# The places of some raw tiles' splits and loads in the first, sixth, seventh and ninth period, and the seventh rotation of down weights one period up, in a fused conditioning, attention and FFN kernel

## The chip, the cores and the metric

One core of one Trainium2 chip. The metric is the device time of one execution in microseconds (us). The kernel before took 1590.42 us, the median of three executions (1587.31, 1590.42 and 1590.79).

## The reference

Four sequences of 512 tokens with 512 channels go through two blocks. `_bi_wkv` is a recurrence over the tokens in both directions, `_L0_attn_ref` an attention by segments with a memory of 128 x 128 per head, `_L0_ffn_ref` a gated FFN whose hidden vector is rotated by a Hadamard transform.

```python
x = x + attn(bi_wkv(x, fside, fside, w, u, cond), Wq, Wk, Wv, Wo, betas)
x = x + ffn(bi_wkv(x, fside, fside, w2, u2, cond), W1, W2, W3)
# bi_wkv: two scans a = a*decay + exp(k)*v and b = b*decay + exp(k) forward, two backward,
#         out = sigmoid(r) * num / den * gain
# attn, per head (16, of 128) and segment (128 tokens):
scores = where(causal_mask, q @ k.T / scale, -inf)
att_dot = softmax(scores) @ v
att_mem = sigma_q @ mem / (sigma_q @ z)
delta = v - sigma_k @ mem / (sigma_k @ z)
mem, z = mem + sigma_k.T @ delta, z + sum(sigma_k)
out = (beta * att_mem + (1 - beta) * att_dot) @ Wo
# ffn: hidden = fwht(silu(x @ W1.T) * (x @ W3.T)); out = hidden @ W2.T
```

## The kernel before

Every engine has its own program, written out by hand; semaphores tie them together. The order inside an engine's program is fixed, so an instruction that waits holds all behind it on that engine.

**Periods.** The attention is a loop over n = 0 to 31 (sequence n // 8, pair of heads n % 8). One turn n is the period n + 1 of this text: n = 0 is the first period, n = 5 the sixth, n = 29 the 30th. In a period TensorE (PE) turns keys and makes scores (`turn_k`, `scores`), turns the attention of the period before (`turn_att`), updates and reads the memory (`update`, `recall`), multiplies probabilities by values (`pv`), and in between multiplies out values (`v_block`, rows `psG<-parts,yh`) and the keys and queries of the next period (`kq_part`, rows `psG<-yh,parts`). Every fourth period (n = 4, 8, ...) is a burst, in which the projection by Wo is made too (`wo`, rows with `ah`).

**Raw tiles.** fp32 products are made in three passes of a high and a low part. The weights come as a stream `STREAM` of tiles of 128 x 1024. The first time that a tile is needed it is loaded raw, in two halves of 256 KB, into `stage` (four buffers, so two tiles; SP, `load_half`), the high part is made by ACT (`split_hi`, L1702; for some tiles by POOL, L2211), the low part by POOL (`split_w`, L2213), and SP saves both (`keep`, `high_k<-parts` and the like). Later uses load the saved parts (`load_w`, `parts<-high_v` and the like, 512 KB each). Tiles lie in a ring of seven places; a load or a split waits (`wait_used`) until PE has used the tile before in its place and its save has landed. `split_hi(upto)`, `split_w(upto)`, `load_w(upto)` and `keep(upto)` go on in the stream up to tile `upto`; `ENDS[n]` is the end of period n's part of it. Tile 4 is the key weight for n = 2 (called k2 here), tile 30 a value weight for n = 8 and 9 (v9), tile 32 a key weight (k8), tiles 40 to 43 are Wo tiles (o12 to o15), tiles 46 and 47 are the value weights that the tenth period uses first (w10, w11), tile 48 a key weight (k10, the keys of n = 10, made in the tenth period).

**Work behind.** Each period has eight slots (`behind(n, k)`). A table `STEPS`, cut by `shared_out` with costs and rooms, says which steps of the recurrence (scans on VectorE, DVE; `yh`: high part of its output by ACT, low part `yl` by POOL) and which of the eight rotations of the down weights fall into which slot. A rotation i loads HA (`load`), adds and subtracts on DVE (`lv0` to `lv3`), makes high and low part HH (ACT, L1776) and HL (DVE, L1238) in `hi` and `lo`, multiplies by a Hadamard matrix on PE (`mult`, function `hadamard`, four matmuls, L872 and L873), copies the result to HO and stores it (ACT, `out_w2`). HH, HL and HO have one buffer each. `hadamard(i)` waits for HH and HL of i, and for the copies of i - 1.

**Waits that the prediction speaks of.** `v_block(0, half, 0)` writes PSUM bank G[half] and waits until ACT has read the queries of n = 1 out of it: `w.wait_ge(a_qm, 2 + half + 1)`, which `relu_kq(1, "q", half, ...)` (L1880) counts up. The value blocks of the seventh period (n = 6, called SWAPPED) are the first for the second sequence and wait for all its `yh` and `yl`.

Of the kernel before, what the change touches and what calls it, by code (L numbers as in the profile page):

```python
# [65 lines left out]
STEPS = [(name, t, cost) for t in range(4, NA) for name, cost in SCAN]  # L66
STEPS += [("hstart", 0, 3000)]
for _i in range(8):
    for name, cost in HADAMARD:
        if name != "mult":  # L70
            STEPS.append((name, _i, cost))
        elif _i > 0:
            if _i == 2:
                STEPS += [(z, 0, c) for z, c in MODULATE[1:]]
            STEPS.append((name, _i - 1, cost))
            if _i == 1:
                STEPS.append(MODULATE[0][:1] + (0, 0))
# [75 lines left out]
SWAPPED = 6  # L153
# [157 lines left out]
def adaln_attn_ffn(nc, xT_d, fT_d, wu_d, wq_d, wk_d, wv_d, wo_d, betas_d,  # L311
# [9 lines left out]
    with ExitStack() as ctx:  # L321
# [1363 lines left out]
        def scalar(e):  # L1685
# [103 lines left out]
            def out_w2(i):  # L1789
                for j in range(2):  # L1790
                    cut = slice(512 * j, 512 * j + 512)
                    w.wait_ge(pe_h, 2 * i + j + 1)
                    w.wait_ge(d_ho, 16 * i)
                    e.activation(HO[:, cut], X[j][:, :], ACT.Copy, scale=RSQ).then_inc(a_ho, 1)
                w.wait_ge(a_ho, 2 * i + 2)
                e.dma_start(w2_s[i].rearrange("p a d -> p (a d)"), HO[:, :]).then_inc(d_ho, 16)
# [10 lines left out]
            def behind(n, k):  # L1807
                for name, i, _ in STEPS[at[0]:UPTO[n, k]]:
                    if name == "nf":
                        load_k(i + 2 if i + 2 < NA else NT)  # L1810
                    elif name == "er":
                        exp_r(i)
                    elif name == "ek":
                        exp_k(after(i))
                    elif name == "eu":
                        exp_u(after(i))
                    elif name == "rc1":
                        load_r(i)
                    elif name == "yh":
                        high_y(i)  # L1820
                        keep_ratio(i)
                    elif name == "hi":
                        high_w2(i)
                        if i == 7:
                            out_w2(6)
                    elif name == "load":
                        load_w2(i)
                    elif name == "mult" and i != 6:
                        out_w2(i)
                    elif name == "zsig":  # L1830
                        z_sigmoid(i)
                    elif name in ("z0", "z1", "z2", "z3"):
                        z_high(i, int(name[1]))
                at[0] = UPTO[n, k]
# [22 lines left out]
            def copy_kq(n, kind, j, bank):  # L1857
                w.wait_ge(pe_k if kind == "k" else pe_q, 2 * n + j + 1)
                w.wait_ge(pe_s, 2 * (n - 1) + j + 1)
                if n == 0:  # L1860
                    w.wait_ge(v_oy, 4)
                e.activation((kT if kind == "k" else qT)[:, j, :], bank[:, :], ACT.Copy).then_inc(  # L1862
                    a_kc if kind == "k" else a_qc, 1)
# [135 lines left out]
            for n in range(NN):  # L1999
                nx, burst = n + 1, is_burst(n)  # L2000
                more = nx < NN
                end, o = ENDS[n], ENDS[n] - 10
# [19 lines left out]
                exp_s(n, 1)  # L2022
                behind(n, 1)
                if n in (SWAPPED, NN - 2):
                    copy_kq(nx, "k", 0, G[0])
                    exp_kq(nx, "k", 0, G[0])
                elif more and not bare:
                    copy_v(n, 0)
                elif not more:
                    sigmoid(0, 0, G[0])  # L2030
# [3 lines left out]
                    exp_u(4)  # L2034
                if burst:
                    copy_v(n, 1)
                if n == SWAPPED:
                    behind(n, 3)
                split_hi(o + 3 if burst else 3 if n == 0 else end if more else end + 1)
                behind(n, 3)  # L2040
                if n == SWAPPED:
# [34 lines left out]
                        copy_kq(nx, "k", j, G[j])  # L2076
                        exp_kq(nx, "k", j, G[j])
                if more:
                    split_hi(5 if n == 0 else end + (3 if n == 3 else 1 if burst else 2))
                    copy_kq(nx, "q", 0, G[0])  # L2080
                    exp_kq(nx, "q", 0, G[0])
                    if n not in (0, 4):
                        split_hi(end + (4 if n == 3 else 3 if burst else 2))
                    copy_kq(nx, "q", 1, G[1])
                    if n == 0:
                        exp_kq(nx, "q", 1, G[1])
                    if n == 4:
                        split_hi(end + 3)
                else:
                    high_h(0, 0)  # L2090
                    high_h(0, 1)
# [100 lines left out]
        def gpsimd(e):  # L2192
# [133 lines left out]
            for n in range(NN):  # L2326
                nx, burst = n + 1, is_burst(n)
                more = nx < NN
                end, o = ENDS[n], ENDS[n] - 10
                if n >= LATE_V:  # L2330
                    scale_v(n)
                behind(n, 0)
                if n > 0:
                    split_w(o + 2 if burst else end + 1 if n == 3 else end - 1 if more else end)
                behind(n, 1)
                behind(n, 2)
                if n == 0:
                    ekv(4)
                    euv(4)
                if n == SWAPPED:  # L2340
                    behind(n, 3)
                split_w(o + 3 if burst else 3 if n == 0 else end if more else end + 1)
                behind(n, 3)
                if burst:
                    split_w(o + 5)
                behind(n, 4)
                split_w(o + 8 if burst else 4 if n == 0 else end + 2 if n == 3 else end + 1 if more else end + 2)
                behind(n, 5)
                if more and n != 4 and nx < LATE_V:
                    scale_v(nx)  # L2350
                if burst:
                    split_w(end)
                if n == 4:
                    scale_v(nx)
                behind(n, 6)
                if burst:
                    split_w(end + 2)
                if more:
                    split_w(5 if n == 0 else end + (4 if n == 3 else 3 if burst else 2))
                else:  # L2360
                    low_h(0, 0)
                    low_h(0, 1)
                behind(n, 7)
# [49 lines left out]
        def sync(e):  # L2413
# [110 lines left out]
            for n in range(NN):  # L2524
# [27 lines left out]
                keep(o + 5 if burst else end + 2 if n == 3 else end)  # L2552
                load_w(o + 9 if burst else 6 if n == 0 else end + (5 if n == 3 else 3))
                behind(n, 5)
                if burst:
                    keep(o + 8)
                    load_w(o + 11)
# [5 lines left out]
                    load_w(o + 13)  # L2563
                if more:
                    keep(5 if n == 0 else end + (4 if n == 3 else 2 if burst else 1))
                    load_w(end + (6 if n == 3 else 4))
                behind(n, 7)
            def load_x(b):
                w.wait_ge(d_x1[b], 16)
# [107 lines left out]
```

## Time and profile before

| | |
|---|---|
| median of three executions | 1590.42 us |
| the profiled execution | 1587.02 us |
| its span | 1585.2 us |
| PE busy | 1542.9 us (97%), 8854 matmuls |
| DVE, ACT, POOL busy | 1214.6 (77%), 781.1 (49%), 615.5 us (39%) |
| prologue, 0 to 60.38 us | PE busy 33.10 us |
| 32 periods, 60.38 to 1068 us | PE busy 997.15 of 1007.62 us |
| FFN, 1068 to 1585.2 us | PE busy 512.67 of 517.20 us |

The span is from the first to the last instruction; 1.8 us of the profiled time lie around it. A period lasts 26 to 29 us, a burst some 49. Matmuls overlap, so PE's busy time is that of the union; a matmul of 512 columns starts 0.23 us after the one before it at full clock. Where PE is idle the timeline says how long before an instruction, and which event came last.

### The profile page before, as it was taken

To read this page: it belongs to the slowest core of one execution; us is meant where nothing else is said; L and a number is where in the kernel's file an instruction comes from. 1 tells how busy PE (TensorE), PEld (TensorE's weight loads), DVE (VectorE), ACT (ScalarE), POOL (GpSimd) and SP (SyncE) were. 2 spreads that over 40 slices of the span, in tenths; PEclk is the share of its full clock that TensorE was granted. 3 is DMA by queue.
4 is the path that set the end of the run, shared out by engine and by line. 5 is a ranking of instruction groups with operands and counts; after the bars stand their busy time and mean duration, and the time that the engine had idled before them with its cause. 6 is when DMAs were issued, how large, how long until landed. Compare 5 with 4: busy or idle time off the path is not lost.

```text
span 1585.2 us, 25420 instructions
## 1 busy us (share of the span) xinstructions
PE 1542.9 (97%) x8854; PEld 1342.2 (85%) x8854; DVE 1214.6 (77%) x2718; ACT 781.1 (49%) x1687; POOL 615.5 (39%) x433
## 2 busy tenths in 40 slices
PE   4899999999999999999999999999999999999999
PEld 2678998898898898898889889889888888888887
DVE  8869968888878778888765764665897888687785
ACT  3556655645526535644645562662554443344442
POOL 3647646262211113222101010143664465666662
PEclk9999999999999999999999999999999999999999
DMA  5357677577485386386278658347211122311111
GB/s 176 123 194 249 236 280 250 195 288 297 176 294 181 134 300 226 113 304 226 97 268 332 209 196 325 103 168 254 90 59 53 58 90 73 107 43 64 54 41 54
DMA packets 113407, 276.62 MB, mean 175 GB/s; under 512 B 11648, under 2 KB 36608, under 8 KB 111872
## 3 DMA queue, kind: packets, MB, share of 16 engines
q1 hardware_dynamic: 94416, 241.96, 42.3%
q10 hardware_dynamic: 18864, 33.04, 6.7%
q8 instruction: 71, 1.16, 0.3%
q14 instruction: 56, 0.46, 0.1%
HBM read 226.71 MB, written 48.25 MB: 173 GB/s over the span
## 4 chain that ended last, share of the span: by engine, by line
PE 88%; DVE 6%; issue 2%; DMA 2%; ACT 1%; POOL 1%; SPq 0%; ACTq 0%; POOLq 0%; DVEq 0%
PE psG L664 16%; PE psG L666 16%; PE psG L665 16%; PE psX L664 4%; PE psX L852 3%; PE psX L665 3%; PE psX L666 3%; PE psX L807 3%; PE psZ L833 3%; PE psZ L824 2%; PE psZ L832 2%; PE psZ L665 2%; PE psY L665 2%; PE psZ L666 2%; PE psZ L664 2%
## 5 line engine op out<-in xcount | busy, mean ns | idle before, releaser
L2213 POOL TENSOR_TENSOR parts<-stage,parts 128x512 fp32r<-128x512 f32 x160 | 235.2, 1492 | 143.0 <-ACT parts L1702 140.6
L664 PE MATMUL psG<-yh,parts 128*128 128x512 f32 x646 | 263.0, 407 | 0.0
L666 PE MATMUL psG<-yh,parts 128*128 128x512 f32 x646 | 253.0, 392 | 0.0
L665 PE MATMUL psG<-yl,parts 128*128 128x512 f32 x646 | 251.8, 390 | 0.0
L2281 POOL TENSOR_TENSOR vs<-v,omb 128x512 f32<-128x512 f32 x64 | 92.9, 1474 | 386.2 <-PE psX L807 210.4
L666 PEld LDWEIGHTS psG<-yh,parts 128*128 128x128 f32 x646 | 121.2, 188 | 26.7
L664 PEld LDWEIGHTS psG<-yh,parts 128*128 128x128 f32 x646 | 121.7, 188 | 21.8 <-issue 0.4
L665 PEld LDWEIGHTS psG<-yl,parts 128*128 128x128 f32 x646 | 121.8, 189 | 21.4
L664 PE MATMUL psG<-ah,parts 128*128 128x256 f32 x448 | 127.1, 284 | 0.2 <-POOL parts L2213 0.2
L665 PE MATMUL psG<-al,parts 128*128 128x256 f32 x448 | 125.2, 280 | 0.0
L666 PE MATMUL psG<-ah,parts 128*128 128x256 f32 x448 | 124.8, 279 | 0.0
L1702 ACT ACTIVATE parts<-stage 128x512 fp32r<-128x512 f32 x152 | 88.0, 623 | 55.1 <-DMA stage<-in_w 15.8
L1862 ACT ACTIVATE kT<-psG 128x512 f32<-128x512 f32 x62 | 37.0, 596 | 152.2 <-PE psG L666 150.8
L1212 DVE RECIPROCAL DBK<-DF 128x128 f32<-128x128 f32 x120 | 107.3, 926 | 0.6
L664 PE MATMUL psG<-parts,yh 128*128 128x512 f32 x240 | 101.1, 421 | 6.5 <-ACT etmp L1880 3.7
L1910 ACT ACTIVATE S<-S,st 128x128 f32<-128x128 f32 x256 | 99.0, 391 | 8.1 <-issue 5.5
L1295 DVE CUSTOM_DVE_ANT_0 S<-psX,mask 128x128 f32<-128x128 f32 x256 | 57.8, 286 | 55.9 <-PE psX L807 55.9
L1307 DVE TENSOR_TENSOR mem<-psZ,mem 128x129 f32<-128x129 f32 x192 | 47.8, 287 | 64.1 <-PE psZ L824 64.1
L666 PE MATMUL psG<-parts,yl 128*128 128x512 f32 x240 | 95.1, 396 | 0.0
L665 PE MATMUL psG<-parts,yh 128*128 128x512 f32 x240 | 94.1, 392 | 0.0
L2289 POOL TENSOR_TENSOR hl<-sg,hh 128x512 fp32r<-128x512 f32 x36 | 51.0, 1416 | 91.8 <-ACT hh L1960 91.8
L664 PEld LDWEIGHTS psG<-ah,parts 128*128 128x128 f32 x448 | 84.2, 188 | 0.4 <-issue 0.3
(279 smaller groups left out, 4241.3 us busy)
## 6 DMA issues: line engine op xcount, KB each, us to landing
parts<-high_o SPq DMA_DIRECT2D x52, 512.0 KB, 6.1
parts<-low_o SPq DMA_DIRECT2D x52, 512.0 KB, 7.6
parts<-high_v SPq DMA_DIRECT2D x36, 512.0 KB, 4.8
parts<-low_v SPq DMA_DIRECT2D x36, 512.0 KB, 6.4
stage<-in_w SPq DMA_DIRECT2D x64, 256.0 KB, 3.0
parts<-high_k SPq DMA_DIRECT2D x23, 512.0 KB, 5.5
parts<-low_k SPq DMA_DIRECT2D x23, 512.0 KB, 6.3
parts<-high_q SPq DMA_DIRECT2D x23, 512.0 KB, 4.5
```

Of the source, the lines that this page charges most:

```text
L664: e.matmul(out, lh, rh, start=first, stop=False, skip_group_check=check)
L665: e.matmul(out, lh, rl, start=False, stop=False, skip_group_check=check)
L666: return e.matmul(out, ll, rh, start=False, stop=last, skip_group_check=check)
L807: m = e.matmul(X[j][:, seg(s)], qT[:, j, seg(s)], kT[:, j, seg(s)], start=True, stop=True)
L1212: e.reciprocal(dbk[:, 128 * j:128 * j + 128], df[:, 128 * j:128 * j + 128]).then_inc(v_rc, 1)
L1295: m = e.tensor_tensor_reduce(S[:, j, seg(s)], X[j][:, seg(s)], mask[:, :], -SCALE, -NEG, ALU.add, ALU.min, st[:, 1, j, s:s + 1])
L1307: e.tensor_tensor(mem[:, j, 0:P + 1], Z[j][:, 258:387], mem0[:, 0:P + 1] if s == 0 else mem[:, j, 0:P + 1], ALU.add).then_inc(v_mem, 1)
L1702: e.activation(hi, raw, ACT.Copy).then_inc(a_wh, 1)
L1910: m = e.activation(S[:, j, seg(s)], S[:, j, seg(s)], ACT.Exp, bias=st[:, 1, j, s:s + 1], scale=-1.0, accum_out=st[:, 2, j, s:s + 1])
L2213: e.tensor_tensor(lo, raw, hi, ALU.subtract).then_inc(p_wl, 1)
L2281: e.tensor_tensor(vs[:, :, j, :].rearrange("p (a b) d -> p a b d", a=2), pick(v[:, :, :, j, 0:P], *HALVES[n]), omb[:, 128 * j:128 * j + 12 ...
L2289: e.tensor_tensor(hl[u % 2][:, j, :], hid(k)[:, :], hh[u % 2][:, j, :], ALU.subtract).then_inc(p_hl, 1)
```

## The change

Four places. (1) First period: ACT splits tile 4 (k2) after the queries of n = 1 are copied out of PSUM, where it did it before them. (2) Sixth and seventh period: ACT and POOL split tile 30 (v9) at the end of the sixth instead of amid the seventh, SP loads tile 32 one place earlier, POOL's `EUV` comes after that split, and in the seventh (and the 31st) ACT does slot 2's work (there `yh` and the last HH) before it copies keys out of PSUM. (3) Ninth period: SP issues the loads of w10 and w11 between saves of the Wo tiles instead of after all four. (4) `mult` of rotation 6 moves from slot 1 of the 31st period to slot 3 of the 30th, with `out_w2(6)`; the steps of rotation 7 that followed (`load`, `lv0` to `lv2`) move one slot back, `lv3` stays.

```diff
@@ -66,10 +66,12 @@
 STEPS = [(name, t, cost) for t in range(4, NA) for name, cost in SCAN]
 STEPS += [("hstart", 0, 3000)]
 for _i in range(8):
+    if _i == 7:
+        STEPS.append(("mult", 6, 300))
     for name, cost in HADAMARD:
         if name != "mult":
             STEPS.append((name, _i, cost))
-        elif _i > 0:
+        elif 0 < _i < 7:
             if _i == 2:
                 STEPS += [(z, 0, c) for z, c in MODULATE[1:]]
             STEPS.append((name, _i - 1, cost))
@@ -1821,11 +1823,9 @@
                         keep_ratio(i)
                     elif name == "hi":
                         high_w2(i)
-                        if i == 7:
-                            out_w2(6)
                     elif name == "load":
                         load_w2(i)
-                    elif name == "mult" and i != 6:
+                    elif name == "mult":
                         out_w2(i)
                     elif name == "zsig":
                         z_sigmoid(i)
@@ -2022,6 +2022,7 @@
                 exp_s(n, 1)
                 behind(n, 1)
                 if n in (SWAPPED, NN - 2):
+                    behind(n, 2)
                     copy_kq(nx, "k", 0, G[0])
                     exp_kq(nx, "k", 0, G[0])
                 elif more and not bare:
@@ -2034,8 +2035,6 @@
                     exp_u(4)
                 if burst:
                     copy_v(n, 1)
-                if n == SWAPPED:
-                    behind(n, 3)
                 split_hi(o + 3 if burst else 3 if n == 0 else end if more else end + 1)
                 behind(n, 3)
                 if n == SWAPPED:
@@ -2076,16 +2075,17 @@
                         copy_kq(nx, "k", j, G[j])
                         exp_kq(nx, "k", j, G[j])
                 if more:
-                    split_hi(5 if n == 0 else end + (3 if n == 3 else 1 if burst else 2))
+                    if n > 0:
+                        split_hi(end + (3 if n == 3 else 1 if burst else 2))
                     copy_kq(nx, "q", 0, G[0])
                     exp_kq(nx, "q", 0, G[0])
                     if n not in (0, 4):
-                        split_hi(end + (4 if n == 3 else 3 if burst else 2))
+                        split_hi(end + (4 if n == 3 else 3 if burst or n == 5 else 2))
                     copy_kq(nx, "q", 1, G[1])
                     if n == 0:
                         exp_kq(nx, "q", 1, G[1])
-                    if n == 4:
-                        split_hi(end + 3)
+                    if n in (0, 4):
+                        split_hi(5 if n == 0 else end + 3)
                 else:
                     high_h(0, 0)
                     high_h(0, 1)
@@ -2337,8 +2337,6 @@
                 if n == 0:
                     ekv(4)
                     euv(4)
-                if n == SWAPPED:
-                    behind(n, 3)
                 split_w(o + 3 if burst else 3 if n == 0 else end if more else end + 1)
                 behind(n, 3)
                 if burst:
@@ -2356,7 +2354,7 @@
                 if burst:
                     split_w(end + 2)
                 if more:
-                    split_w(5 if n == 0 else end + (4 if n == 3 else 3 if burst else 2))
+                    split_w(5 if n == 0 else end + (4 if n == 3 else 3 if burst or n == 5 else 2))
                 else:
                     low_h(0, 0)
                     low_h(0, 1)
@@ -2552,6 +2550,10 @@
                 keep(o + 5 if burst else end + 2 if n == 3 else end)
                 load_w(o + 9 if burst else 6 if n == 0 else end + (5 if n == 3 else 3))
                 behind(n, 5)
+                if n == 8:
+                    load_w(o + 11)
+                    keep(o + 6)
+                    load_w(o + 12)
                 if burst:
                     keep(o + 8)
                     load_w(o + 11)
@@ -2563,7 +2565,7 @@
                     load_w(o + 13)
                 if more:
                     keep(5 if n == 0 else end + (4 if n == 3 else 2 if burst else 1))
-                    load_w(end + (6 if n == 3 else 4))
+                    load_w(end + (6 if n == 3 else 5 if n == 5 else 4))
                 behind(n, 7)
             def load_x(b):
                 w.wait_ge(d_x1[b], 16)
```

On ACT, at the end of the first period, before (stage0 and stage1 hold k2; qT, etmp0 and etmp1 belong to the queries of n = 1):

```order
L1702 ACTIVATE parts<-stage0 128x512
L1702 ACTIVATE parts<-stage1 128x512
L1862 ACTIVATE qT<-psG0 128x512
L1880 ACTIVATE etmp0<-psG0 128x512
L1871 ACTIVATE etmp0<-etmp0 128x512
L1862 ACTIVATE qT<-psG1 128x512
L1880 ACTIVATE etmp1<-psG1 128x512
L1871 ACTIVATE etmp1<-etmp1 128x512
L1720 ACTIVATE ER<-ER 128x512
```

and in the change:

```order
L1862 ACTIVATE qT<-psG0 128x512
L1880 ACTIVATE etmp0<-psG0 128x512
L1871 ACTIVATE etmp0<-etmp0 128x512
L1862 ACTIVATE qT<-psG1 128x512
L1880 ACTIVATE etmp1<-psG1 128x512
L1871 ACTIVATE etmp1<-etmp1 128x512
L1704 ACTIVATE parts<-stage0 128x512
L1704 ACTIVATE parts<-stage1 128x512
L1722 ACTIVATE ER<-ER 128x512
```

Two splits moved from ahead of six instructions to behind them; ER is still last.

On ACT, across the border of the sixth and the seventh period, before (stage0 and stage1 hold v9; `ah`, `bet`, `omb` and S belong to the seventh):

```order
L1910 ACTIVATE S,st<-S,st 128x128 x4
L1702 ACTIVATE parts<-stage0 128x512
L1702 ACTIVATE parts<-stage1 128x512
L1910 ACTIVATE S,st<-S,st 128x128 x4
L1862 ACTIVATE kT<-psG0 128x512
L1880 ACTIVATE etmp0<-psG0 128x512
L1871 ACTIVATE etmp0<-etmp0 128x512
L1768 ACTIVATE yh1<-OY 128x512
L1745 DMA kx0<-in_fT 128x512
L1862 ACTIVATE kT<-psG1 128x512
```

and in the change:

```order
L1910 ACTIVATE S,st<-S,st 128x128 x8
L1770 ACTIVATE yh1<-OY 128x512
L1862 ACTIVATE kT<-psG0 128x512
L1880 ACTIVATE etmp0<-psG0 128x512
L1871 ACTIVATE etmp0<-etmp0 128x512
L1747 DMA kx0<-in_fT 128x512
L1862 ACTIVATE kT<-psG1 128x512
```

The two splits are gone from here (they stand ahead of `qT<-psG1`, ten instructions earlier), and yh stands ahead of the three instructions on psG0.

On PE in the 31st period, before, the four matmuls of rotation 6 with one row on either side (`psZ1<-v,kn` ends `update`, psG1 is the second half of the next keys):

```order
L824 MATMUL psZ1<-v,kn 128x129
L872 MATMUL psX0<-HH,had 128x512
L873 MATMUL psX0<-HL,had 128x512
L872 MATMUL psX1<-HH,had 128x512
L873 MATMUL psX1<-HL,had 128x512
L664 MATMUL psG1<-yh1,parts 128x512
```

On PE in the 30th period, between `recall` of the second segment and the second half of a value block, in the change:

```order
L834 MATMUL psZ1<-mem,sk 128x129
L835 MATMUL psZ1<-mem,sq 128x129
L874 MATMUL psX0<-HH,had 128x512
L875 MATMUL psX0<-HL,had 128x512
L874 MATMUL psX1<-HH,had 128x512
L875 MATMUL psX1<-HL,had 128x512
L666 MATMUL psG1<-parts,yh1 128x512
L667 MATMUL psG1<-parts,yh1 128x512
L668 MATMUL psG1<-parts,yl1 128x512
```

The four matmuls of rotation 6 have left the 31st period, where `psG1<-yh1,parts` now follows `psZ1<-v,kn` at once, and stand behind `recall` and ahead of the value block.

## Rows read from the trace of the kernel before

**Rows 1.** waits of PE, whole span: us in total, times, longest
```profile
PE psG L664 <- ACT etmp L1880: 3.7, 1, 3.7
...
PE psG L664 <- POOL yl L2238: 2.5, 1, 2.5
PE psX L872 <- DVE HL L1238: 1.3, 1, 1.3
```

**Rows 2.** timeline of PE, first period: start, us, what [idle before]
```profile
81.59 0.39 PE L666 MATMUL psG<-yh,parts 128*128 128x512 f32 x1
85.71 0.58 PE L664 MATMUL psG<-parts,yh 128*128 128x512 f32 x1 [3.73 <-ACT etmp L1880]
...
89.43 0.39 PE L664 MATMUL psG<-parts,yh 128*128 128x512 f32 x1
```

**Rows 3.** windows: us; PE, PEld, DVE, ACT, POOL busy; PEclk; DMA; GB/s
```profile
85.70:89.50 3.80, 3.79 (x10) 2.98 (x11) 0.00 (x0) 2.65 (x5) 1.42 (x3) 0.55 0.96 357
```

**Rows 4.** timeline of ACT, end of the first period
```profile
82.69 0.63 ACT L1702 ACTIVATE parts<-stage 128x512 fp32r<-128x512 f32 x1 [4.98 <-DMA stage<-in_wk]
```

**Rows 5.** timeline of DVE, first and second period
```profile
80.65 1.70 DVE L1365 SCALAR_TENSOR_TENSOR sk<-kT,etmp 128x512 f32<-128x512 f32 x1
...
96.33 0.69 DVE L1365 SCALAR_TENSOR_TENSOR sq<-qT,etmp 128x512 f32<-128x512 f32 x1
...
100.27 0.46 DVE L1307 TENSOR_TENSOR mem<-psZ,mem 128x129 f32<-128x129 f32 x2
```

**Rows 6.** timeline of POOL, end of the first period
```profile
91.71 1.29 POOL L2213 TENSOR_TENSOR parts<-stage,parts 128x512 fp32r<-128x512 f32 x1
```

**Rows 7.** timeline of PE, second and seventh period
```profile
100.74 0.38 PE L832 MATMUL psZ<-mem,sk 128*128 128x129 f32 x2
...
260.96 0.47 PE L664 MATMUL psG<-parts,yh 128*128 128x512 f32 x1 [2.50 <-POOL yl L2238]
```

**Rows 8.** timeline of ACT, seventh period
```profile
248.31 0.60 ACT L1862 ACTIVATE qT<-psG 128x512 f32<-128x512 f32 x1 [0.99 <-PE psG L666]
...
256.71 0.57 ACT L1862 ACTIVATE kT<-psG 128x512 f32<-128x512 f32 x1
...
258.33 0.61 ACT L1768 ACTIVATE yh<-OY 128x512 fp32r<-128x512 f32 x1
```

**Rows 9.** timeline of POOL, seventh period
```profile
254.91 3.47 POOL L2213 TENSOR_TENSOR parts<-stage,parts 128x512 fp32r<-128x512 f32 x2 [5.33 <-ACT parts L1702]
259.02 1.68 POOL L2238 TENSOR_TENSOR yl<-OY,yh 128x512 fp32r<-128x512 f32 x1 [0.63 <-ACT yh L1768]
```

**Rows 10.** timeline of PE, 30th and 31st period
```profile
1001.18 0.47 PE L664 MATMUL psG<-parts,yh 128*128 128x512 f32 x1
...
1026.01 0.39 PE L664 MATMUL psG<-yh,parts 128*128 128x512 f32 x1
...
1029.73 0.47 PE L872 MATMUL psX<-HH,had 128*128 128x512 f32 x1 [1.28 <-DVE HL L1238]
```

**Rows 11.** timeline of DVE, 30th and 31st period
```profile
1001.78 1.23 DVE L1238 TENSOR_TENSOR HL<-HA,HH 128x1024 fp32r<-128x1024 f32 x1 [3.05 <-ACT HH L1776]
...
1028.41 1.23 DVE L1238 TENSOR_TENSOR HL<-HA,HH 128x1024 fp32r<-128x1024 f32 x1 [2.64 <-ACT HH L1776]
```

**Rows 12.** timeline of ACT, 31st period
```profile
1025.70 0.58 ACT L1862 ACTIVATE kT<-psG 128x512 f32<-128x512 f32 x1
...
1027.33 1.04 ACT L1776 ACTIVATE HH<-HA 128x1024 fp32r<-128x1024 f32 x1
```

**Rows 13.** timelines of PE, tenth period, and of SP, ninth period
```profile
355.28 0.47 PE L664 MATMUL psG<-parts,yh 128*128 128x512 f32 x1 [0.22 <-issue]
...
362.24 0.40 PE L664 MATMUL psG<-yh,parts 128*128 128x512 f32 x1
...
344.15 1.00 SPq L2455 DMA_DIRECT2D parts<-low_k  x1
```

**Rows 14.** DMA issues, 343.7 to 346 us: count, KB, us to landing
```profile
parts<-low_k SPq DMA_DIRECT2D x1, 512.0 KB, 15.1
```

## Prediction

> **What bounds the kernel now.** I read the page first: PE is busy for 1542.9 of 1585.2 us, so only what PE waits for can be won. Next the waits of PE over the whole span: behind the prologue there are three above 1 us, one each, of 3.7, 2.5 and 1.3 us [rows 1]. Then the timelines of PE around these three, to see where they lie, and of ACT, POOL and DVE at the same times, to see what each engine did instead. The first lies at the end of the first period [rows 2], the second in the seventh [rows 7], the third in the 31st [rows 10]. The change touches just these places, and the ninth period, where the next one has a wait of 0.22 us [rows 13]. All else that follows is tied to PE's progress, so I let later work move along with PE.
>
> **A, first period.** PE's last matmul on the queries of n = 1 starts at 81.59 and the value block behind it at 85.71, released by etmp [rows 2]. That is ACT's relu of these queries, and ACT stood before it at the first raw half of k2: 4.98 us idle until its DMA landed, and 82.69 when it began [rows 4]. With the splits behind the queries' six instructions, ACT takes half 0 as soon as PE has made it. The second half of the queries is 12 matmuls of 0.23 us, so half 0 is ready near 79.1; a copy and a relu of 0.6 us each make it free at 80.3, before PE gets there at 81.82. For half 1 ACT can copy at 82.0; its relu also waits for sk, DVE's op of 1.70 us from 80.65, done at 82.35 [rows 5]; it ends near 83.2, and PE comes to half 1 at 81.82 + 12 x 0.23 = 84.6. So the wait goes whole: 85.71 - 81.82 = 3.9 us. Behind the wait the granted clock was 0.55 of full on the mean of 85.7 to 89.5, that is mostly its lower level of 1.2 GHz [rows 3]: nine starts took 89.43 - 85.71 = 3.72 us [rows 2], where nine at 0.23 and a first one 0.1 longer take 2.17. Without 3.73 us of idleness before it I expect no fall of the clock: another 1.55 us. A is worth -5.4 us.
>
> What pays for it: k2 is split about 1 us later (behind ACT's exp of half 1, near 83.7, not at 82.69), and PE begins the second period 5.4 us earlier. k2 and q2 are used only in the middle and at the end of the second period. But POOL's last low part of q2, at 91.71 to 93.0 [rows 6], ended before DVE's sq at 96.33 (0.69 us). Now it runs at about 90.2 to 91.5 (POOL no longer waits for ER there), and sq comes at 96.33 - 5.4 = 90.9. The like op at 80.65 took 1.70 us, with POOL busy beside it [rows 5]. So sq and all behind it on DVE are late by between 0 and 1.0 us; I take the overlap, 0.5. DVE's mem begins at 100.27 and takes 0.46 for two halves, the first done near 100.5, and PE reads it at 100.74 [rows 5, 7]: 0.2 us of slack, so PE waits 0.3 us, between 0 and 0.8. Estimate +0.3. The Trainium skill, SBUF — State Buffer, section "SBUF: two separate sides", says that DVE and GpSimd share a port pair as an exclusive lock, whichever starts first holding it for its whole instruction. By that rule sq waits out POOL's op and runs 0.5 us late, and by the nearest row 1.0 us; the wait of PE would be 0.3 or 0.8.
>
> **B, seventh period.** The value block begins at 260.96 behind 2.50 us of idleness, released by yl [rows 7]. POOL made yl from 259.02, when yh had come, and yh stood at 258.33 behind ACT's three instructions on the keys, which began at 256.71 [rows 8, 9]. POOL itself was at v9 until 254.91 + 3.47 = 258.38. Now both are out of the way: v9's two splits on ACT leave (1.04 us earlier), and yh goes first, at 256.71 - 1.04 = 255.7. It is done at 256.3, yl at 256.3 + 1.3 to 1.7 = 257.6 to 258.0, and PE wants it at 260.96 - 2.50 - 0.16 (matmuls overlap) = 258.3. The keys' relu, which the block waits for too, ends near 257.5. So the wait goes whole, -2.6 us, between -2.2 and -2.66.
>
> The split that moved costs ACT 1.04 us ahead of q1's copy at 248.31, before which ACT was idle for 0.99 [rows 8]: 0.05 us, for which scores of half 1 would wait, hidden by those of half 0 (0.9 us). POOL's v9 now ends near 251; then EUV, needed in slot 7 only. No cost. If v9's raw halves landed later than 247.2, ACT and with it q1, scores and all of the seventh period would wait for them one for one.
>
> **C, rotation 6.** In the 30th period PE would now do the four matmuls at the place of the row at 1001.18. They wait for HL of 6, which DVE makes from 1001.78 to 1003.01, being itself released by HH on ACT [rows 10, 11]. Nothing in the change makes this earlier: HH stands behind the copies of rotation 5 and a value copy. PE's idleness there is new: 1003.1 - 1001.3 = 1.8 us (the like place in the 31st began 0.09 after HL ended). In the 31st period the four matmuls (1.0 us) are gone, so PE reaches rotation 7 at 1028.3 - 1.0 = 1027.3 in the old time. HH of 7 now goes ahead of the keys' copies, at 1025.70 and not 1027.33 [rows 12], so HL is ready at 1029.64 - 1.63 = 1028.0, and PE waits 0.7 us where it waited 1.3. Sum: 1.8 + 0.7 - 1.3 = +1.2 us. Bounds: 0 if HL of 6 were early enough, 2.0 if the order on ACT brings nothing. Behind the waiting matmuls in the 30th stand the value block and turn_p; ACT and DVE wait for these but have slack of 0.8 us and more, so nothing is added. A clock fall is not counted: the wait of 2.50 us had none behind it (0.47 us for its first matmul, as ever) [rows 7].
>
> **D, ninth period.** The block at 355.28 waits 0.22 us for w10 and w11 [rows 13]. w11 now has two saves of 1 MB less ahead of it, so it comes earlier and the 0.22 goes: -0.3 us with the overlap. The Trainium skill, DMA: Bandwidth & Descriptors, section "Queues, rings and completion order", says that descriptors are consumed in ring order; that is why issuing earlier helps, and the sum would be the same without it.
>
> **Sum:** -5.4 + 0.3 - 2.6 + 1.2 - 0.3 = -6.8 us. Against the profiled execution, 1587.0, that is 1580.2 (span 1578.4). The median shown is 3.4 us higher, 1590.4, and gives 1583.6; two of four executions lie at 1587 and two at 1590.6. I put 1583.0.
>
> **Rivals.** (1) As summed, -5 to -8.8: 0.63. (2) Part of A and B is given back: the clock falls all the same, or POOL, DVE or transfers in the second to fifth period don't follow PE by 5.4 us. For it speaks that DVE is full there and its op grew from 0.69 to 1.70 us beside POOL [rows 5]; against it, that PE hardly waits there now. Worth 1.6 (clock) + 2 = 3.6: -3.2 us, 0.2; a quarter of it within 0.2%. (3) The change doesn't do what it says: v_block waits for something else at 82 us, as the split v3 whose low part is POOL's. Then A is nearly 0: -1.5 us, 0.08, and no change to be measured. (4) The other side: in the ninth period the loads between the saves hold up SP. w11 waits for the save of o12, and saves of o14 and o15 and the load of k10 stand behind it. k10's low part was issued at 344.15 and took 15.1 us [rows 13, 14], landing at 359.3; PE uses it at 362.24 [rows 13], 2.9 us of slack. Each us beyond costs one; it takes 6.8 + 3.2 + 2.9 = 13 us of delay before the kernel is slower by 0.2%. The bytes ahead of k10 are the same, so I expect none; 0.05, at +4 us. (5) C costs nothing and all else holds: -8.0, 0.04.
>
> **Numbers.** 0.2% (3.2 us) is about what a measurement of this kernel can tell from no change. Faster by more: 0.63 + 0.15 + 0.04 = 0.82; within: 0.05 + 0.08 = 0.13; slower: 0.05. The range goes from the profiled time less 8.4 (1578.6) to the median less 2.8 (1587.6); what lies outside is (3), (4) and the tails.
>
> **What would show it.** PE's wait for etmp gone and PEclk 1.00 from 80 to 90 us; no wait for yl near 250; a new wait for HL of 1.8 us near 994 and one of 0.7 near 1021; none for `issue` near 347; mem L1309 as releaser in the second period with 0.3 us. Wrong would be: k2 landing so late that POOL runs into DVE's chain for more than 1 us, or a wait for transfers in the tenth period.

## The result, and the profile after

The changed kernel takes 1579.93 us (median of 5 runs, 1579.76 to 1580.68). The kernel before, in the same comparison, takes 1590.42 us (5 runs, 1587.31 to 1590.79). The ratio is 0.994, with a 95% interval of 0.9926 to 0.9955: faster by 0.6%, an effect under 2% but clear of 1. The time forecast was 1583.0 us, with a range of 1578.6 to 1587.6; the time lies inside, 3.1 us below the forecast. The profiled execution took 1580.52 us with a span of 1578.7 us, where the sum of the prediction had 1580.2 and 1578.4.

A period is counted here from the first matmul of one period's first block to that of the next, so that the lengths and the prologue add up, but for the last stretch, to the span. From the two timelines of PE:

| stretch | before, us | after, us | change | foretold |
|---|---|---|---|---|
| prologue | 60.38 | 60.01 | -0.37 | nothing |
| 1st period | 32.46 | 26.89 | -5.57 | -5.4 |
| 2nd | 26.08 | 26.61 | +0.53 | +0.3 |
| 7th | 28.84 | 26.10 | -2.74 | -2.6 |
| 10th | 26.58 | 26.09 | -0.49 | -0.3 |
| 15th | 26.38 | 27.21 | +0.83 | nothing |
| 30th and 31st | 27.02 + 24.00 | 29.83 + 22.37 | +1.18 | +1.2 |
| span | 1585.2 | 1578.7 | -6.5 | -6.8 |

The waits of PE in the kernel after, over the whole span (us in total, times, longest); these answer to [rows 1]:

```profile
PE psX L874 <- issue: 2.3, 2, 1.7
PE psZ L834 <- DVE mem L1309: 1.9, 5, 0.8
```

The waits of 3.7 us for etmp and 2.5 us for yl are gone. In their place stand two at the Hadamard matmuls (line 874, that was 872) and a longer list for mem. The timeline of PE after shows them one by one (start, duration, and in brackets the idle time before):

```profile
95.22 0.49 PE L834 MATMUL psZ<-mem,sk 128*128 128x129 f32 x2 [0.27 <-DVE mem L1309]
...
505.37 0.49 PE L834 MATMUL psZ<-mem,sk 128*128 128x129 f32 x2 [0.85 <-DVE mem L1309]
...
995.37 0.47 PE L874 MATMUL psX<-HH,had 128*128 128x512 f32 x1 [1.68 <-issue]
...
1023.19 0.47 PE L874 MATMUL psX<-HH,had 128*128 128x512 f32 x1 [0.59 <-issue]
```

The window of 80 to 90 us after (us; PE, PEld, DVE, ACT, POOL busy; PEclk; DMA share; GB/s) is full, at full clock, where the kernel before had 0.55 behind its wait [rows 3]:

```profile
80.00:90.00 10.00, 10.00 (x61) 8.74 (x60) 4.79 (x19) 5.79 (x13) 7.21 (x9) 1.00 0.86 311
```

ACT at the end of the first period after, against [rows 4]: the queries' copy and relu stand at once behind PE, and the splits of k2 come last.

```profile
78.92 0.60 ACT L1862 ACTIVATE qT<-psG 128x512 f32<-128x512 f32 x1 [1.42 <-PE psG L668]
79.41 0.59 ACT L1880 ACTIVATE etmp<-psG 128x512 f32<-128x512 f32 x1
...
82.15 0.59 ACT L1880 ACTIVATE etmp<-psG 128x512 f32<-128x512 f32 x1
...
83.32 1.14 ACT L1704 ACTIVATE parts<-stage 128x512 fp32r<-128x512 f32 x2
```

POOL and DVE in the second period after, against [rows 5, 6]: sq starts 0.58 us after POOL's low part of q2 and takes 1.26 us, not 0.69. mem is late by as much as its slack doesn't cover, and PE waits 0.27 us.

```profile
89.81 1.30 POOL L2213 TENSOR_TENSOR parts<-stage,parts 128x512 fp32r<-128x512 f32 x1
```

```profile
90.39 1.26 DVE L1367 SCALAR_TENSOR_TENSOR sq<-qT,etmp 128x512 f32<-128x512 f32 x1
...
94.91 0.46 DVE L1309 TENSOR_TENSOR mem<-psZ,mem 128x129 f32<-128x129 f32 x2
```

In the seventh period after, yh and yl are early enough (against [rows 8, 9], which had them at 258.33 and 259.02 in a period that began 5.4 us later in the span):

```profile
250.33 0.61 ACT L1770 ACTIVATE yh<-OY 128x512 fp32r<-128x512 f32 x1
```

```profile
251.02 1.29 POOL L2238 TENSOR_TENSOR yl<-OY,yh 128x512 fp32r<-128x512 f32 x1 [4.35 <-ACT yh L1770]
```

In the 30th and 31st period after, each Hadamard matmul starts 0.1 us behind the end of HL, though the view names only "issue" as its releaser; the timeline of DVE (against [rows 11]) says what was really late:

```profile
994.04 1.22 DVE L1240 TENSOR_TENSOR HL<-HA,HH 128x1024 fp32r<-128x1024 f32 x1 [3.05 <-ACT HH L1778]
...
1021.86 1.23 DVE L1240 TENSOR_TENSOR HL<-HA,HH 128x1024 fp32r<-128x1024 f32 x1 [1.03 <-ACT HH L1778]
```

On SP in the ninth period after, w11's load is issued at 334.35, ahead of two saves, and k10's low part at 339.65 (against [rows 13]); no wait follows in the tenth:

```profile
334.35 0.32 SPq L2452 DMA_DIRECT2D parts<-high_v  x1
...
339.65 0.68 SPq L2453 DMA_DIRECT2D parts<-low_k  x1
```

### The profile page after: what moved, and what is told of

Its sections match the earlier page's. It is cut to its first block, busy times and chain, and to the rows that moved or that the text cites. A ratio compares the mean times of both kernels' runs of the same rounds, so it can differ in the third digit from the quotient of the medians.

```text
span 1578.7 us, 25420 instructions
## 1 busy us (share of the span) xinstructions
PE 1542.7 (98%) x8854; PEld 1341.6 (85%) x8854; DVE 1217.6 (77%) x2718; ACT 781.4 (49%) x1687; POOL 614.3 (39%) x433
## 4 chain that ended last, share of the span: by engine, by line
PE 89%; DVE 6%; issue 2%; ACT 1%; DMA 1%; POOL 0%; ACTq 0%; SPq 0%; DVEq 0%; POOLq 0%
PE psG L666 16%; PE psG L668 16%; PE psG L667 16%; PE psX L854 4%; PE psX L666 4%; PE psX L668 3%; PE psX L667 3%; PE psX L809 3%; PE psZ L835 3%; PE psZ L826 3%; PE psZ L834 2%; PE psY L667 2%; PE psZ L667 2%; PE psZ L668 2%; PE psZ L666 2%
```

## The experiments

Two questions stood after this. One is whether the four parts have the prices of the table. The other is why the medians differ by 10.5 us where the two profiled executions differ by 6.5. Experiments 1 to 4 put one part each into the kernel before. Their times are compared with 30 executions of it (median 1588.42 us, 1585.42 to 1591.06).

**1. Part A alone.** The splits of k2 behind the queries on ACT:

```diff
-                    split_hi(5 if n == 0 else end + (3 if n == 3 else 1 if burst else 2))
+                    if n > 0:
+                        split_hi(end + (3 if n == 3 else 1 if burst else 2))
...
-                    if n == 4:
-                        split_hi(end + 3)
+                    if n in (0, 4):
+                        split_hi(5 if n == 0 else end + 3)
```

> Of the change, the part in the first period alone (k2 split behind the queries). Own theory: the wait for etmp and the low clock behind it go, a wait of 0.3 us for mem comes in the second period; span 1585.2 - 5.6 + 0.4 = 1580.0 us, ratio 0.9965 or lower. Rival, that part of the gain is given back in the second to fifth period: span 1582 or more. Second question: the median of the kernel before (1590.4) lies 3.4 us above its profiled execution, while the changed kernel's executions lie within 0.9 us; if the spread comes from the wait in the first period, it is gone here (executions within 1 us, median near 1582).

Measured: 1583.74 us (6 runs, 1582.56 to 1585.3), ratio 0.9972 (0.9961 to 0.9983). First period 26.90 us, second 26.60: as expected. But the span was 1581.5, only 3.7 below that of before, since its seventh period took 30.38 us and not 28.84, with the same wait for yl before it. The timeline of PE of this kernel:

```profile
255.97 0.76 PE L664 MATMUL psG<-parts,yh 128*128 128x512 f32 x1 [2.49 <-POOL yl L2239]
```

The wait is that of [rows 7], but the matmul behind it takes 0.76 us, not 0.47. The clock fell here, where the prediction had counted on no fall. Two more points of the expectation failed: the ratio is above 0.9965, and the six executions are spread over 2.7 us, not within 1. So the first period is not the only source of the spread.

**2. Part B alone** (sixth and seventh period):

```diff
+                if n == SWAPPED:
+                    behind(n, 2)
...
-                if n == SWAPPED:
-                    behind(n, 3)
...
-                        split_hi(end + (4 if n == 3 else 3 if burst else 2))
+                        split_hi(end + (4 if n == 3 else 3 if burst or n == 5 else 2))
```

with the like edits on POOL and SP.

> The part in the sixth and seventh period alone (v9 split earlier, yh ahead of the keys' copies). Own theory: the wait of 2.5 us for yl goes, nothing else moves: span 1585.2 - 2.7 = 1582.5 us. Rival: yl is as late as before for another reason (OY late once the first period is not shortened), then 1584 to 1585. Second question: if the spread of the kernel before comes from this wait (the clock falling behind it in some executions), its executions lie within 1 us here.

Measured: 1584.99 us (11 runs, 1582.58 to 1586.85), ratio 0.9978 (0.997 to 0.9987); span 1582.7, first period 32.28, seventh 26.10. The period shrinks by 2.74 us, the median by 3.4. The executions are spread over 4.3 us, where the second question had 1: the seventh period alone isn't the source of the spread either.

**3. Part C alone** (the step "mult" of rotation 6 in the 30th period, HH of 7 ahead of the keys):

```diff
+    if _i == 7:
+        STEPS.append(("mult", 6, 300))
...
-        elif _i > 0:
+        elif 0 < _i < 7:
...
+                if n == NN - 2:
+                    behind(n, 2)
```

> The part on rotation 6 alone (its matmuls in the 30th period, HH of rotation 7 ahead of the keys' copies in the 31st). Own theory: slower by 1.2 us: a wait of 1.8 us in the 30th, 0.7 instead of 1.3 in the 31st; span 1586.4. Rival, that the part pays: the new wait is covered and the 1.3 us go, span 1583.9.

Measured: 1590.29 us (12 runs, 1588.12 to 1591.45), ratio 1.0012 (1.0003 to 1.0021): a loss. 30th period 29.85 us with a wait of 1.68, 31st 22.34 with one of 0.59: +2.83 - 1.66 = +1.17 us, the 1.2 of the prediction.

**4. Part D alone** (ninth period, SP):

```diff
+                if n == 8:
+                    load_w(o + 11)
+                    keep(o + 6)
+                    load_w(o + 12)
```

> The part in the ninth period alone (loads of w10 and w11 between the saves). Own theory: the wait of 0.22 us in the tenth goes, span 1584.8 to 1585.0. Rival, that SP's queue is held up by the wait for the save of o12 and a later load comes late: a wait on `issue` or a load in the tenth period, span 1586 or more.

Measured: 1587.82 us (11 runs, 1585.64 to 1589.3), ratio 0.9997 (0.9989 to 1.0006). By times this can't be told from no change. The trace has the effect: tenth period 26.09 us without a wait, against 26.58. The span was 1587.4 us, where 1584.8 to 1585.0 was expected; it lies in the rival's range, but not by the rival's wait. The seventh period again took 30.43 us behind a wait of 2.49, and the 15th 27.13.

The four medians give 4.7 + 3.4 - 1.9 + 0.6 = 6.8 us together, against 8.5 for the whole change from the same 1588.42. By its interval each of the four is known to some 1.5 us, so this neither confirms nor refutes that the parts add up; the prices by part below rest on the profiles.

**5. The changed kernel with rotation 6 back in the 31st period**, HH of 7 still early. Against the kernel after:

```diff
-    if _i == 7:
-        STEPS.append(("mult", 6, 300))
...
-        elif 0 < _i < 7:
+        elif _i > 0:
...
+                        if i == 7:
+                            out_w2(6)
```

> The changed kernel with rotation 6 back in the 31st period, HH of rotation 7 still ahead of the keys' copies. Own theory: the wait of 1.7 us in the 30th goes; in the 31st HH of 7 must wait for rotation 6's matmuls (over 0.2 us after exp ends), so HL is ready near the time PE comes: a wait of 0.3 instead of 0.6; span 1578.7 - 2.0 = 1576.7 us (less 0.8 if the fifteenth period's wait for mem doesn't come). Rival: HL or HO is later than that and the wait of 1.3 us stands again, span 1578.2.

Measured: 1578.19 us (5 runs, 1577.62 to 1580.36), ratio to before 0.9938 (0.9925 to 0.9952), span 1576.5. The 30th period is back at 27.02 us and the 31st takes 23.40: with HH early the wait before rotation 7 is 0.24 us, as PE of this kernel shows:

```profile
1021.10 0.47 PE L872 MATMUL psX<-HH,had 128*128 128x512 f32 x1 [0.24 <-DVE HL L1238]
```

The highest run of this kernel, 1580.36, is 2 us above the others; it has no profile. The move itself costs 52.20 - 50.42 = 1.8 us, and the earlier HH, which came with it, gives 0.6 of this back.

**6 and 7. A wait of chosen length at the old place.** ACT makes some copies that nobody needs (into `pad`) before the relu for which PE waits, so that the same value block stands still; short 5 copies, long 8. Against the kernel after:

```diff
                     copy_kq(nx, "q", 0, G[0])
+                    if n == 0:
+                        for i in range(8):
+                            e.activation(pad[:, :], G[0][:, :], ACT.Copy).then_inc(a_c, 1)
+                            w.wait_ge(a_c, 5 + i)
                     exp_kq(nx, "q", 0, G[0])
```

> The changed kernel with 5 further copies of psG0 into an unused tile, one after another, on ACT between the copy and the relu of the first queries, so that PE waits at the same place for some 1.7 us. Own theory, that the clock falls behind a long wait only: the wait, PEclk 1.00 behind it, first period 26.9 + 1.8 = 28.7 us. Rival, that any wait there brings the lower clock: PEclk near 0.55 behind it, 30.2 us.

> The same with 8 further copies, so that PE waits for some 3.6 us, as long as in the kernel before. Own theory, that the wait alone brings the fall of the clock: PEclk near 0.55 behind it, first period 26.9 + 3.8 + 1.5 = 32.2 us. Rival, that something else of the kernel before did (DMA, the raw tile): PEclk 1.00, 30.7 us.

Measured: short 1581.89 us (one run), span 1580.0, first period 28.85; long 1585.01 us (one run), span 1583.2, first period 32.38. The first timeline and the two windows are of the short one, the second set of the long one:

```profile
84.03 0.47 PE L666 MATMUL psG<-parts,yh 128*128 128x512 f32 x1 [1.68 <-ACT etmp L1880]
```

```profile
84.00:86.00 2.00, 1.97 (x9) 1.66 (x10) 0.16 (x1) 1.97 (x4) 0.00 (x0) 1.00 1.02 414
86.00:88.00 2.00, 2.00 (x11) 1.65 (x10) 0.00 (x0) 1.74 (x4) 1.16 (x1) 1.00 0.54 209
```

```profile
85.38 0.47 PE L666 MATMUL psG<-parts,yh 128*128 128x512 f32 x1 [3.57 <-ACT etmp L1880]
```

```profile
86.00:88.00 2.00, 2.00 (x6) 1.61 (x5) 0.00 (x0) 1.97 (x5) 0.00 (x0) 0.50 0.25 95
88.00:90.00 2.00, 2.00 (x7) 1.56 (x7) 0.00 (x0) 1.09 (x3) 1.80 (x2) 0.69 0.01 4
```

Behind 1.68 us of idleness 11 matmuls start in 2 us, as at full clock; behind 3.57 us, 6, at a granted clock of 0.50. The period is longer than 26.89 by 1.96 us in the short one (1.68 of it the wait) and by 5.49 in the long one: 3.57 of wait and 1.9 of slower matmuls. So the clock fall comes back with the wait alone, without the old order of the splits. Each of the two is one execution.

**8. GpSimd's split of q2 out of DVE's way.** Against the kernel after, POOL holds it until DVE's first mem of the second period:

```diff
                 behind(n, 0)
+                if n == 1:
+                    w.wait_ge(v_mem, 8)
```

> The changed kernel with POOL's split of q2 held back in the second period until DVE has done the first mem, by a wait at the head of POOL's second period. Own theory, that the second period is 0.5 us longer than before since POOL's op runs beside DVE's sq: sq takes 0.69 us, the wait of 0.27 us for mem goes, the second period takes 26.1 us. Rival, that DVE was late for another reason: sq still 1.2 us or more, 26.6 us. By either, POOL's work may meet other DVE ops later, in the third period.

Measured: 1579.42 us (one run), span 1577.6. The timelines of POOL and DVE of this kernel:

```profile
95.02 0.62 POOL L2211 TENSOR_SCALAR parts<-stage 128x512 fp32r<-128x512 f32 x1 [7.08 <-DVE mem L1309]
```

```profile
90.53 0.69 DVE L1367 SCALAR_TENSOR_TENSOR sq<-qT,etmp 128x512 f32<-128x512 f32 x1
```

sq is back at 0.69 us and the second period at 26.07, 0.54 less. The split ran 7 us later and nobody waited for it. The remaining 0.6 us of the span comes from the 15th period, 26.47 here against 27.21, which this edit doesn't touch (below).

**9 to 11. Three more profiles of the kernel before**, unchanged, to see whether its own executions differ at the seventh period. The expectations call each of them a look.

> The kernel before, unchanged, profiled once more. Theory 1 (behind the wait of 2.5 us for yl in the seventh period the clock falls in some executions and not in others, at a price of 1.54 us): the wait is 2.4 to 2.6 us in every look, the seventh period is 28.8 us or 30.4 us long with nothing between, and in a look with 30.4 the window behind the wait has a granted clock under 1.00; the first period is 32.3 to 32.5 us in all looks. Theory 2 (the fall came from what parts A or D change ahead of it): the seventh period is 28.8 us in every look of this kernel.

> The kernel before, unchanged, a second look. As for the first look: theory 1 has a seventh period of 28.8 or of 30.4 us, by chance; theory 2 has 28.8 us always. Over the three looks theory 1 expects at least one of 30.4 us (two of four profiles with this wait had it).

> The kernel before, unchanged, a third look. Theory 1: a seventh period of 28.8 or of 30.4 us. Theory 2: 28.8 us. Both: a look with 30.4 us has a span 1.5 us longer than one with 28.8 us, where nothing else differs.

Measured: 1590.7, 1586.85 and 1590.06 us; spans 1588.9, 1585.0 and 1588.2. The seventh period took 30.43, 28.84 and 30.42 us. Experiment 9, timeline of PE and windows:

```profile
86.28 0.76 PE L664 MATMUL psG<-parts,yh 128*128 128x512 f32 x1 [4.22 <-ACT etmp L1880]
...
262.79 0.74 PE L664 MATMUL psG<-parts,yh 128*128 128x512 f32 x1 [2.51 <-POOL yl L2238]
```

```profile
88.00:90.00 2.00, 2.00 (x6) 1.52 (x6) 0.00 (x0) 0.95 (x2) 0.96 (x2) 0.50 0.98 393
90.00:92.00 2.00, 2.00 (x7) 1.52 (x6) 0.00 (x0) 0.00 (x0) 1.92 (x3) 0.50 0.97 274
...
264.00:266.00 2.00, 2.00 (x7) 1.51 (x7) 0.00 (x0) 0.00 (x0) 1.92 (x3) 0.50 0.99 394
```

Experiment 10, timeline of PE, and the windows behind the first and the second wait:

```profile
85.38 0.77 PE L664 MATMUL psG<-parts,yh 128*128 128x512 f32 x1 [3.68 <-ACT etmp L1880]
...
260.50 0.47 PE L664 MATMUL psG<-parts,yh 128*128 128x512 f32 x1 [2.51 <-POOL yl L2238]
```

```profile
89.00:92.00 3.00, 3.00 (x15) 2.49 (x14) 0.00 (x0) 0.00 (x0) 2.83 (x4) 1.00 0.77 226
...
262.00:264.00 2.00, 2.00 (x17) 1.87 (x16) 0.75 (x5) 1.09 (x2) 1.92 (x3) 1.00 1.01 388
```

One kernel, one wait of 2.51 us, once with the clock at 0.50 behind it and once at 1.00. Theory 2 falls. But both theories were wrong on the first period: it was to be 32.3 to 32.5 us in every look, and was 34.13, 32.25 and 33.76. Its wait was 4.22, 3.68 and 3.89 us, and the fall behind it cost 1.7 us in experiment 10 and 3.0 in the others. The price goes with how long the clock stays down: from 90 to 92 us it is still at 0.50 in experiment 9, while in experiment 10 it is at 1.00 from 89 us on. ACT shows where the length of the wait comes from: it waits for the raw half of k2, and for a different time in each execution. Experiment 9, then 10:

```profile
83.88 1.28 ACT L1702 ACTIVATE parts<-stage 128x512 fp32r<-128x512 f32 x2 [5.93 <-DMA stage<-in_wk]
```

```profile
82.53 0.63 ACT L1702 ACTIVATE parts<-stage 128x512 fp32r<-128x512 f32 x1 [4.93 <-DMA stage<-in_wk]
```

**12. Both improvements together:** the changed kernel with the edits of 5 and 8.

> The changed kernel with the rotation of the sixth down weights back in the thirty-first period, and GpSimd's split of the second period's queries held until the first mem of that period is written. If the 0.5 us of the second period is the lock between VectorE's sq and GpSimd's split (theory), it goes here as it went with the hold alone: second period 26.1 us instead of 27.0, span 1575.6 us (1576.5 less 0.9), time 1577.4 us. Rival: the hold only shifts the collision to another period, the span stays at 1576.5 us and the time at 1578.2 us.

Measured: 1578.38 us (5 runs, 1577.98 to 1579.21), ratio 0.9937 (0.9924 to 0.9951), span 1576.1; 1577.4 and 1575.6 were expected. The second period is 26.08 us, 0.93 less than in 5, as expected; the span is only 0.4 less, since 5 had the FFN some 0.6 us shorter in its profile. By times 5 and 12 can't be told apart, and the rival's time, 1578.2, is as near as one can measure; it is the period that speaks against the rival. Both medians lie below the lowest run of the changed kernel, 1579.76.

## Why the prediction was right, and where its size was off

**A.** Right in mechanism and in size for the profile shown: 26.89 us, -5.57 against -5.4. The relus of the two halves ended at 80.0 and 82.7 us (foretold 80.3 and 83.2), and no fall followed. Experiments 1 and 7 (long) show both halves: taking the splits away takes all of it, putting a wait of 3.57 us back brings 5.5 us back. Too small was "Without 3.73 us of idleness before it I expect no fall of the clock: another 1.55 us". What the fall costs is not one number, and this is the term of the sum that was mis-sized. Seven executions of kernels with the old order (before in four, and experiments 2 to 4) have the first period at 32.25 to 34.13 us. With 26.90 and their waits taken off, 1.6 to 1.9 us stay in five of them and 3.0 in two, where 1.55 was forecast. Over the four of the kernel before A is worth 33.15 - 26.89 = 6.3 us.

**The meeting on DVE and POOL** was right by mechanism, +0.53 against +0.3. That sq pays for POOL's low part is shown by experiment 8. The size can be read from many meetings in these traces. It is in each what was left of POOL's tensor_tensor when sq began, less about 0.14 us. Six of them: in the second period 0.72 left and +0.57 (after), 0.69 and +0.56 (experiment 1), 0.81 and +0.67 (6), 1.13 and +0.99 (5); in the 15th 1.20 and +1.06 (after), 0.37 and +0.23 (before). One of nine like meetings with `vs` in the later periods of the kernel before, on POOL and DVE, has 0.94 left and +0.81:

```profile
813.50 2.55 POOL L2281 TENSOR_TENSOR vs<-v,omb 128x512 f32<-128x512 f32 x2 [23.96 <-PE psX L807]
...
815.11 1.50 DVE L1365 SCALAR_TENSOR_TENSOR sq<-qT,etmp 128x512 f32<-128x512 f32 x1
```

So the price could have been read for sq itself before the change was made, and not bounded by sk's 1.70 us. The rule that the prediction weighed (the Trainium skill, SBUF — State Buffer, section "SBUF: two separate sides": the one that starts first holds the shared pair for its whole instruction) agrees with all of them, up to these 0.14 us. So the lower of the two prices was right, while the bound of 0.8 was almost reached in experiment 5, where PE waits 0.68.

**B.** The wait went whole, -2.74 us against -2.6. What failed is the sentence "A clock fall is not counted: the wait of 2.50 us had none behind it (0.47 us for its first matmul, as ever) [rows 7]." It stands under C, but B rests on it as well: B has no term for a clock fall. It took one execution for all. In seven executions with this wait (2.49 to 2.51 us in each) the period took 28.84 to 28.86 us in three and 30.38 to 30.43 in four, nothing between: 1.57 us for a fall that comes or doesn't. B is therefore worth 2.74 or 4.3 us; over the four executions of before, 29.63 - 26.10 = 3.5.

**C.** Right: waits of 1.68 and 0.59 us (foretold 1.8 and 0.7), +1.18 us in the sum (1.2). No fall followed these, as assumed. The releaser named for them is "issue"; that it is HL follows from the 0.1 us between its end and the matmul, in both periods. Experiment 3 has the loss by itself, 5 has it taken back.

**D.** Right in sign: the wait is gone in all profiles with the new order, the tenth period at 26.09 us. The old one was 26.58, 26.68, 26.95 and 27.11 in the four executions of before, so it is worth 0.7 us on the mean, against 0.3. k10 came in time; the rival of a late k10 had no place.

**Not foreseen:** the 15th period, +0.83 us. In the kernel after, the timelines of ACT, POOL and DVE have:

```profile
500.35 1.27 ACTq L1941 DMA_DIRECT2D omb<-beta_s  x1
```

```profile
502.47 1.29 POOL L2226 TENSOR_TENSOR EUV<-EU,kx 128x512 f32<-128x512 f32 x1 [7.03 <-ACT EU L1716]
```

```profile
502.56 1.75 DVE L1367 SCALAR_TENSOR_TENSOR sq<-qT,etmp 128x512 f32<-128x512 f32 x1
```

and in the kernel before:

```profile
508.93 0.44 ACTq L1941 DMA_DIRECT2D omb<-beta_s  x1
```

```profile
510.22 1.29 POOL L2226 TENSOR_TENSOR EUV<-EU,kx 128x512 f32<-128x512 f32 x1 [6.21 <-ACT EU L1714]
```

```profile
511.14 0.92 DVE L1365 SCALAR_TENSOR_TENSOR sq<-qT,etmp 128x512 f32<-128x512 f32 x1
```

The issue of one small DMA took 0.83 us longer on ACT's queue. EU comes later by as much, POOL's EUV starts just ahead of sq and not well before it, sq takes 1.75 us, mem is late and PE waits 0.85. Of the fourteen profiles, three have the long issue: after (1.27), experiment 4 (1.22, period 27.13 us) and experiment 1 (1.41). The others have 0.44 to 0.60 and periods of 26.38 to 26.55. In experiment 1 EU was so late that sq began before EUV: sq took 0.68 us, POOL's EUV, 0.05 us behind it, took 1.79 instead of 1.29, and the period was 26.12 us, the shortest of all. All three have part A or D in them, but five other profiles with both parts have the short issue, so it is no fixed effect of the change. Whether a part makes it likelier isn't shown, and what makes it long is open: in the eighth period the like issue takes 1.02 to 2.07 us in thirteen of the fourteen profiles, three of the four of before among them.

**Where the 10.5 us came from.** The four profiled executions of before have a mean span of 1586.8, and the one of after 1578.7: 8.1 us. By periods: 6.26 (1st) + 3.53 (7th) + 0.74 (10th) - 0.53 (2nd) - 0.74 (15th, from 26.47) - 1.14 (30th and 31st) = 8.1. So the missing part of the gain is the share of clock falls and of late transfers that the profiled execution of before happened not to have. The rest, to 10.5, is the comparison's own five runs of before, whose median (1590.42) is at the upper end of 1585.42 to 1591.06; against 1588.42 the gain is 8.5. (Two further sets of nine executions of before have medians of 1588.25 and 1588.74.) The prediction saw the two kinds of execution ("two of four executions lie at 1587 and two at 1590.6") and put its time between them, without asking whether the change would remove what sets them apart. It does: the runs of after lie within 0.9 us, and a time worked out from the profiled execution alone (1580.2) would have been 0.3 off. That the span forecast from it came so near (1578.4, measured 1578.7) is in part luck: the unforeseen +0.83 of the 15th period stands against -0.37 of the prologue and -0.3 by which the periods of the change did better than their terms.

## What to carry to other kernels

When the executions of a kernel fall into two groups, find what they differ in before costing a change: here it was whether the clock fell behind an idle stretch of 2.5 us, and how long it stayed down behind one near 4, and a change that takes the idleness away takes most of the spread with it (5.6 us over 30 executions of before, 0.9 over five of after, 2.7 over five in experiment 5). A step moved to an earlier period is worth nothing while its input stays late: four matmuls, 1 us together, brought 1.8 us of waiting with them. Where a DVE instruction with two SBUF inputs begins beside one of POOL's, count what is left of the latter, and hold POOL's if nobody waits for it.

## What the runs showed of the hardware

- In the periods: behind a wait of 1.28 to 1.68 us of PE the granted clock stayed at 1.00 in every profile that has such a wait. Behind 2.49 to 2.51 us it fell to its lower level of 1.2 GHz in four of seven. Behind 3.57 to 4.22 us it fell in all eight. The wait is the same in the seven; what sets them apart is open.
- In the prologue the length of the wait doesn't order the falls. Experiment 4 has one behind 1.94 us, experiment 1 none behind 3.31; PE and the window behind it, experiment 4 first:

```profile
32.17 2.96 PE L686 MATMUL psX<-oys,wr 128*128 128x512 f32 x4 [1.94 <-DVE oys L1218]
```

```profile
33.00:36.00 3.00, 3.00 (x5) 1.22 (x4) 3.00 (x5) 1.40 (x4) 0.00 (x0) 0.51 0.00 0
```

```profile
32.53 1.98 PE L686 MATMUL psX<-oys,wr 128*128 128x512 f32 x4 [3.31 <-DVE oys L1218]
```

```profile
32.50:38.00 5.50, 5.47 (x17) 3.34 (x18) 5.50 (x8) 3.01 (x7) 0.00 (x0) 1.00 0.02 4
```

- A fall cost 1.57 us behind the shorter wait of the periods, and 1.6 to 1.9 or 3.0 us behind the longer one.
- sq on DVE took 0.69 us alone and up to 1.75 beside POOL's tensor_tensor: longer by what was left of that instruction, less 0.14 us.
- The issue of one and the same DMA on ACT's queue, in the 15th period, took 0.44 to 0.60 us in eleven profiles and 1.22 to 1.41 us in three.
